# First attention of a two-block MetaFormer: the weighted sums of two steps issued together

## The reference

```python
q, k, v = split(einsum('oc,bct->bot', qkv_w, normed) + qkv_b)        # 8 images, 8 heads of 16 channels, 1024 places
weight = softmax(einsum('bct,bcs->bts', q * scale, k * scale), axis=-1)
a = einsum('bts,bcs->bct', weight, v)
out = einsum('oc,bct->bot', proj_w, xf + a) + proj_b
```

## Time and profile before

| | us |
|---|---|
| median of 3 runs | 2825.33 |
| lowest and highest of the runs | 2821.86, 2828.52 |
| span of the profiled execution, first to last instruction | 2707.0 |
| TensorE matmuls busy in it | 2312.7 |
| VectorE busy | 1793.9 |
| ScalarE busy | 1084.6 |
| GpSimd busy | 693.1 |

### The profile page before, as it was taken

How to read it: one execution, slowest core, us unless ns; L and a number is a source line. 1 busy time by engine, 2 the same in 40 slices (tenths; PEclk the granted TensorE clock), 3 DMA queues, 4 the chain that set the end, 5 groups by cost and what they waited for, 6 DMA issues and landing times. The chain is left out here.

```text
span 2707.0 us, 34742 instructions
## 1 busy us (share of the span) xinstructions
PE 2312.7 (85%) x10504; PEld 1124.5 (42%) x10504; DVE 1793.9 (66%) x2968; ACT 1084.6 (40%) x1467; POOL 693.1 (26%) x700
## 2 busy tenths in 40 slices
PE   5759999999999997873999479999999766199994
PEld 2412222222222322552666235555555344177773
DVE  5859888878878822442666599999999565122224
ACT  4611767667657685220222023323323343133330
POOL 1230000000000001774666200000000167445552
PEclk9855999999999998766999589999999866599996
DMA  3464224224223001325553400000000011444425
GB/s 145 158 160 63 25 40 64 25 41 64 25 41 48 18 1 52 98 84 162 176 176 112 133 0 1 0 0 0 0 0 1 28 43 50 150 154 153 152 91 199
DMA packets 91038, 198.31 MB, mean 73 GB/s; under 512 B 20128, under 2 KB 25120, under 8 KB 88736
## 3 DMA queue, kind: packets, MB, share of 16 engines
q1 hardware_dynamic: 71584, 155.04, 22.2%
q0 software_dynamic: 19328, 41.72, 4.3%
HBM read 123.54 MB, written 72.75 MB: 73 GB/s over the span
## 5 line engine op out<-in xcount | busy, mean ns | idle before, releaser
L552 DVE TENSOR_REDUCE mx<-bank 128x1 f32<-128x512 f32 x1024 | 633.7, 681 | 123.2 <-PE bank L434 123.1
L537 ACT ACTIVATE P<-bank 128x1024 f32<-128x1024 f32 x512 | 496.2, 1021 | 326.2 <-PE bank L486 325.9
L434 PE MATMUL bank<-ks,qs 96*128 96x512 bf16 x1024 | 370.1, 414 | 34.6 <-DMA ks<-qk_parts 29.9
L1201 POOL DMA_INDIRECT results<-yo,places x312 | 300.7, 964 | 258.9 <-DVE yo L1191 181.4
L486 PE MATMUL bank<-qs,ks 99*128 99x512 bf16 x1024 | 308.8, 386 | 10.0 <-issue 5.6
L1379 PE MATMUL bank<-pad_v,taps 128*128 128x512 f32 x704 | 316.6, 599 | 0.8 <-ACT pad_v L1558 0.8
L1001 POOL DMA_INDIRECT dispatched<-rows,places x256 | 255.8, 999 | 134.1 <-issue 81.3
L1135 PE MATMUL bank<-xt,rec 128*128 128x512 f32 x624 | 284.7, 599 | 4.0 <-DVE xt L1171 4.0
L466 PE MATMUL bank<-P,vt 128*32 128x512 f32 x2048 | 274.3, 608 | 0.7 <-ACT P L537 0.7
L1591 DVE SCALAR_TENSOR_TENSOR dw<-pad_k,weights,dw 128x1024 f32<-128x1024 f32 x192 | 245.4, 1278 | 0.0
L1591 DVE SCALAR_TENSOR_TENSOR dw<-pad_q,weights,dw 128x1024 f32<-128x1024 f32 x192 | 245.4, 1278 | 0.0
(11 more groups left out here) (211 smaller groups left out, 2548.7 us busy)
## 6 DMA issues: line engine op xcount, KB each, us to landing
rec<-e_rec SPq DMA_DIRECT2D x39, 578.0 KB, 3.8
xr<-dispatched SPq DMA_DIRECT2D x78, 260.0 KB, 3.9
y<-results SPq DMA_DIRECT2D x64, 256.0 KB, 4.3
qk_parts<-parts SPq DMA_DIRECT2D x16, 768.0 KB, 4.8
qs<-qk_parts SPq DMA_DIRECT2D x96, 128.0 KB, 6.0
ks<-qk_parts SPq DMA_DIRECT2D x96, 128.0 KB, 6.6
rec<-folded SPq DMA_DIRECT2D x39, 258.0 KB, 2.8
v_turned<-vt SPq DMA_DIRECT2D x8, 1024.0 KB, 3.9
```

The source lines that it names most:

```text
L434: pe.matmul(bank[:, slot, :], qs[0:KB, par, h, c * C:(c + 1) * C], ks[0:KB, par, h, half * HALF:(half + 1) * HALF], start=True, stop=True) ...
L537: act.activation(P[:, x % SLOTS, :], bank[:, 2 * pair:2 * pair + 2, :] .rearrange("p a t -> p (a t)"), ACT.Exp).then_inc(probs_ready, 1)
L552: dve.tensor_reduce(mx[:, k // 2, k % 2:k % 2 + 1], bank[:, slot, :], AX.X, ALU.max).then_inc(unit_freed, 1)
L1201: pool.indirect_dma_start(yd_dram, bass.IndirectOffsetOnAxis(places[:, p, q:q + 1], 0), yo[:, p, q, :], None).then_inc(sent[p], 16)
```

## The change

The weighted sums of two steps are issued together at the end of each even step: `weigh` of e - 2, then of e - 1. At step 0 of an image they are those of steps 30 and 31 of the image before, and the last two come at the end of the stage. `P` gets eight slots, four steps' worth, and ScalarE waits for the sum of e - 4 instead of e - 2. The reciprocal is made in `den` itself, `rden` goes, and VectorE's shuffle waits until GpSimd has used the earlier one (`a_ready`) instead of until the earlier Ln is done.

```diff
--- before.py
+++ after.py
@@ -295,7 +295,7 @@
 
 
 STEPS = 32
-SLOTS = 4
+SLOTS = 8
 
 
 def units_of(prev, more):
@@ -336,7 +336,6 @@
     nm_parts = sb("nm_parts", [32, 3, C], BF16)
     o = sb("o", [C, HALF], F32)
     den = sb("den", [C, HALF], F32)
-    rden = sb("rden", [C, HALF], F32)
     a = sb("a", [C, 2, T], F32)
     ones_set, rows_loaded, v_loaded = sem("ones_set"), sem("rows_loaded"), sem("v_loaded")
     qk_loaded = [sem("qk0_loaded"), sem("qk1_loaded")]
@@ -495,13 +494,16 @@
                                 rows(b if k else b + 1, k, slot)
                             else:
                                 project(before, k, slot)
-                    if e:
-                        weigh(b, par, e - 1)
-                    elif prev:
-                        weigh(before, 1 - par, STEPS - 1)
+                    if e % 2 == 0 and (e or prev):
+                        for back in (2, 1):
+                            if e:
+                                weigh(b, par, e - back)
+                            else:
+                                weigh(before, 1 - par, STEPS - back)
 
             def last():
-                weigh(B - 1, (B - 1) % 2, STEPS - 1)
+                for back in (2, 1):
+                    weigh(B - 1, (B - 1) % 2, STEPS - back)
                 pe.wait_ge(unit_freed, LAST)
                 for n in range(2):
                     project(B - 1, n, 5 + n)
@@ -520,15 +522,15 @@
 
                 act.wait_ge(den_ready, b * 4 + q + 1)
                 act.wait_ge(a_ready, b * 4 + q)
-                act.activation(rden[:], den[:], ACT.Ln).then_inc(den_logged, 1)
+                act.activation(den[:], den[:], ACT.Ln).then_inc(den_logged, 1)
                 act.wait_ge(den_logged, b * 4 + q + 1)
-                act.activation(rden[:], rden[:], ACT.Exp, scale=-1.0).then_inc(rden_ready, 1)
+                act.activation(den[:], den[:], ACT.Exp, scale=-1.0).then_inc(rden_ready, 1)
 
             def body(b, before, par, base, prev, more):
                 for e in range(STEPS):
                     image, q = (b, e // 8 - 1) if e >= 8 else (before, 3)
 
-                    act.wait_ge(pv_done, b * STEPS + (e - 1 if prev else max(e - 1, 0)))
+                    act.wait_ge(pv_done, b * STEPS + (e - 3 if prev else max(e - 3, 0)))
                     if e % 8 == 1 and (prev or e >= 8):
                         numerators(image, q)
                     for pair in range(2):
@@ -571,7 +573,7 @@
             def sums(b, q):
 
                 dve.wait_ge(o_copied, b * 4 + q + 1)
-                dve.wait_ge(den_logged, b * 4 + q)
+                dve.wait_ge(a_ready, b * 4 + q)
                 dve.sem_inc(held, 1)
                 dve.stream_shuffle(den[:], o[:], [CH + i % CH for i in range(32)]).then_inc(den_ready, 1)
 
@@ -617,7 +619,7 @@
                 if used is not None:
                     pool.wait_ge(unit_filled, used)
                 g, n = q // 2, q % 2
-                pool.tensor_tensor(a[:, g, n * HALF:(n + 1) * HALF], o[:], rden[:], ALU.mult).then_inc(a_ready, 1)
+                pool.tensor_tensor(a[:, g, n * HALF:(n + 1) * HALF], o[:], den[:], ALU.mult).then_inc(a_ready, 1)
 
             def first():
                 pool.memset(ks[KB:KM, :, :, :], 1.0).then_inc(ones_set, 1)
```

## The result

The changed kernel takes 2896.1 us (median of 4 runs, 2891.2 to 2898.5) where the kernel before takes 2823.8. The ratio is 1.0254, with a 95% interval from 1.0237 to 1.0271: 72 us slower, and 2895 had been forecast.

The account below looks back on a forecast made before the run. VectorE's chain with TensorE through three PSUM slots was taken to bound the middle images. Losses of 44.8 + 14.3 + 10.9 = 70 us, on the median of 2825.3 us, gave 2895 us, range 2868 to 2912.

Parts of the forecast that it names:

- The chain through three slots: Middle images: eight units wait on VectorE through three PSUM slots, 0.40 us lost per two steps, 44.8 us; chance 0.82.
- The formula: Time of a step's TensorE-VectorE-TensorE links: 2.93 + 0.60 (n - 4) us for n units; 4.33 us to the double sum.
- The second sum: Second weighted sum of a joined pair on TensorE: taken as 0.92 us, bounds 0.85 and 1.00.
- rival 1: Joined sums save 0.18 us of entry and exit per join, VectorE's backlog absorbed: 23 us less, 2802 us; chance 0.08.
- The shuffle: VectorE's shuffle of the sums, amid eight units: 0.62 us shows, 0.53 more than before, 27 times, 14.3 us.
- The last image: No units there; ScalarE idles during double sums: 5.16 us for two steps, +0.73 over 15 windows, 10.9 us.
- rival 3: TensorE's clock falls to 1.2 GHz in the last image: 33 us on top, 2928 us; chance 0.07.
- P slots, in-place reciprocal, a_ready: Eight P slots, the reciprocal in place and VectorE's new wait ahead of the shuffle: all costed at zero.
- The bounds: Inside the forecast: second sum -9 to +10 us, shuffle -14 to +3 us, giving 2872 to 2911 us.
- rival 2: Gain and loss of the joined sums nearly cancel, as with a VectorE pitch near 0.50: 2820 to 2831 us; chance 0.03.

Follow-up runs that it names:

- the experiment: Changed kernel with single weighted sums in the last image alone: 2764.2 us against 2706.7 for the kernel before, ratio 1.0216.
- second profile of before: The kernel before, unchanged, profiled once more: span 2831.0 us, run 2833.1 us, attention stage 785.1 us.
- first profile: The kernel before, unchanged, as profiled for the prediction: span 2707.0 us, attention stage 787.2 us.
- the experiment with 256 columns: Each maximum taken over 256 of 512 columns: in the kernel before 2772.9 us, ratio 0.9782; in the changed kernel 2774.1 us, ratio 0.9793.

## Why the prediction was right

**The chain through three slots.** This was the step that decided the sign, and it holds in each of its links. The formula's 4.33 us to the double sum measured 4.32. The size test (reductions shortened: the loss falls from 72 us to 1, and from 68.8 to 5.6 in the stage) and the slots test (two slots: the order of the middle images turns round, 119.2 to 118.8) were made to break it and didn't. The reason in one line: the weighted sum is the only time in which VectorE catches up, three slots let it be at most three reductions behind, and a double sum offers the same three reductions twice the time while the eight units between must go at VectorE's pitch.

**The second sum.** This term was a little off: 0.92 had been taken, the two together measure 1.86 where one alone takes 1.00, so the second costs 0.86. The lower bound of 0.85 was the better guess: in the double sum at 704.81 the weights of the second half are loaded 0.45 us after those of the first and the next ones 0.43 us later (704.81, 705.26, 705.69), so the nearest row's 0.46 held some cost of going in that a second sum doesn't pay. It makes windows of 6.18 us and not 6.25, a loss of 0.32 each and not 0.40: 36 us in 112 windows, not 44.8. The gain side of rival 1 was real, 0.22 us a window, and was outweighed.

**The shuffle.** Forecast 0.62 where it shows, measured 0.62 (2.47 us over four). With the 0.09 off that the kernel before pays, an image should lose 16 x 0.32 + 4 x 0.53 = 7.24 us; measured are 108.07 - 100.42 = 7.65.

**The border between two images.** The rest holds a term that the sum didn't have. At step 0 the first unit waits for `base + max(index - 2, 0)` reductions, so for all of the image before, and not for all but two, as the units after it do. With a sum at the end of each step there was next to nothing to wait for: the window across the border takes 6.45 us before, as the others with five units do. In the changed kernel it takes 7.39 instead of their 6.78, 0.6 us an image (TensorE's timeline; the last reduction ends at 690.25):

```profile
688.74 0.60 PE L485 MATMUL bank<-qs,ks 99*128 99x512 bf16 x2
690.38 0.60 PE L433 MATMUL bank<-ks,qs 96*128 96x512 bf16 x2 [1.04 <-DVE mx L554]
```

Some of the ordinary windows lose 0.24 to 0.26 us and not 0.32, which brings the sum to 7.65. The kernel with double sums at the odd steps has one right ahead of the border, and its image takes 105.04 us where 105.6 were expected. No run changes this wait alone.

**The last image.** Forecast 10.9 us, 5.16 a window; measured 8.4 in the experiment (from the projection on, which leaves out the first six steps), 5.09 a window. The clock stayed at its 2.4 GHz level there, so rival 3 didn't occur in that image; its mechanism did at the turns. The stretch of the last image in the changed kernel, columns as in the earlier trace rows, has 54.63 us of TensorE and a granted clock of 1.00:

```profile
1020.00:1088.00 68.00, 54.63 (x306) 14.23 (x305) 6.54 (x14) 51.08 (x59) 5.20 (x7) 1.00 0.01 1
```

**The turns.** Not in the sum at all: 2.0 and 4.1 us more than in the second profile of before, 6.1 us together. Against the first profile they are 3.1 and 2.2, 5.2 together. It happened to fill most of what the cheaper second sum left. The stage as a whole went from 785.1 to 853.9 us, +68.8 (+66.7 against the first profile's 787.2), against 70 forecast; the median moved by 72.3. The agreement to 1 us in the total is therefore partly luck; the terms are each good to 1 to 9 us.

**P slots, in-place reciprocal, a_ready.** Costed at nothing, measured as nothing (0.999, 0.9979 to 1.0001).

**Slips that did no harm.** The bounds don't add up as written: 2895 + 10 + 3 is 2908; the 2911 has half of the runs' spread in it and the 2872 hasn't. And rival 1 gave a pitch of 0.50 us for its gain of 23 us, but by the forecast's own sum 4 x 0.10 only cancels the 0.40 of loss, which is rival 2; a gain needs a shorter pitch, as the experiment with 256 columns had.

## What to carry to other kernels

Joining work to save a switch also joins the work in between. Ask what the piece that is taken out was hiding: count the buffers between the two engines, multiply by the slower one's pitch, and that is all it can catch up in one gap, however long the gap. Before joining, look at which unit waits for its slot; here putting the producer's units first, at no cost in buffers, took that wait out of the steps with single sums and was worth 0.8%; of the join's 72 us it gave back 37.

## What the runs showed of the hardware

A second group of four f32 matmuls on 32-column tiles, right behind a first that accumulates in the same bank, costs 0.86 us where a lone one costs 1.00 plus 0.10 ahead of it. The turn of a hardware loop cost TensorE a wait of 1.8 to 3.9 us without a releaser, shorter by what stood in its queue ahead of the turn, and in joined kernels, where the packet of instructions after the next starts 6.6 to 7.5 us and not over 20 us behind the turn, a second one of 2.0 to 2.8. Behind these waits the granted clock was at the 1.2 GHz level for some microseconds (0.50 from 804 to 808 us), and a double sum took 3.57 us instead of 1.86.
